# Attention and MLP kernel on one core: MLP weights split into f16 rows and turned by crossbar transposes instead of on TensorE

## The reference

```python
xn = layernorm(x)                                # x: [1, 2048, 512]
y  = x + attention(xn, Wq, Wkv, Wo, bo) + ffn(xn, gate, up, down)
# attention: 16 heads of 32, 4 key/value heads, causal, ALiBi bias
# ffn: W = lut[4-bit codes] * scales[row, block of 32]; gate, up: [4096, 512], down: [512, 4096]
inter = gelu_tanh(xn @ Wg.T) * (xn @ Wu.T);  ffn = inter @ Wd.T
```

## Time and profile before

| | us |
|---|---|
| median of 3 executions (1735.28 to 1737.32) | 1736.85 |
| the profiled execution | 1738.06 |
| its span in the profile | 1736.2 |
| TensorE busy in the span | 1666.9 (96%) |
| VectorE busy | 1312.1 (76%) |
| ScalarE busy | 1067.0 (61%) |
| GpSimd busy | 935.9 (54%) |

### The profile page before, as it was taken

One profiled execution on the slowest core, in us unless ns is written; L12 is line 12 of the kernel. 1 busy time (PEld: TensorE's weight loads), 2 busy tenths in 40 slices (PEclk: granted clock), 3 DMA queues, 4 the chain that ended last, 5 costly groups with the idle time before them and its releaser, 6 DMA issues.

```text
span 1736.2 us, 30755 instructions
## 1 busy us (share of the span) xinstructions
PE 1666.9 (96%) x10337; PEld 830.9 (48%) x10337; DVE 1312.1 (76%) x2782; ACT 1067.0 (61%) x1788; POOL 935.9 (54%) x807
## 2 busy tenths in 40 slices
PE   4989999999999999999999999999999999999998
PEld 3764444444444444444444444444444444444443
DVE  6767778777777777777777778777777778777755
ACT  2336757575666757575766757575767657575650
POOL 3304637465665747465655747464656647464650
PEclk9999999999999999999999999999999999999999
DMA  6761020202021020202021020202020120202135
GB/s 195 197 188 44 15 74 18 76 26 71 18 62 38 23 79 17 75 27 75 17 72 26 26 76 17 75 27 76 18 76 19 28 74 17 76 27 82 32 102 181
DMA packets 95843, 106.86 MB, mean 62 GB/s; under 512 B 38288, under 2 KB 63768, under 8 KB 93992
## 3 DMA queue, kind: packets, MB, share of 16 engines
q1 hardware_dynamic: 91368, 99.27, 20.6%
q10 hardware_dynamic: 4320, 5.64, 1.0%
HBM read 69.60 MB, written 22.42 MB: 53 GB/s over the span
## 4 chain that ended last, share of the span: by engine, by line
PE 74%; DVE 8%; issue 6%; ACT 5%; DMA 0%; POOL 0%; SPq 0%; POOLq 0%; DVEq 0%; ACTq 0%
PE up_ps L1233 16%; PE down_ps L1213 16%; PE gate_ps L1233 15%; PE o_ps L1276 8%; PE score_ps L1267 8%; PE max_ps L1245 4%; PE turn_ps L1245 3%; ACT p L1395 2%; DVE mxp L1526 2%; PE l_ps L1276 2%; ACT wh L354 1%; PE max_ps L347 1%; DVE score_ps L1511 1%; DVE gl L1482 1%; DVE acc L1473 1%
## 5 line engine op out<-in xcount | busy, mean ns | idle before, releaser
L1668 POOL TENSOR_TENSOR plo<-p,phi 128x512 f16<-128x512 f32 (+1 forms) x576 | 661.0, 1158 | 317.6 <-ACT phi L1402 316.3
L1395 ACT ACTIVATE p<-score_ps,pshift 128x512 f32<-128x512 f32 (+1 forms) x576 | 381.5, 662 | 284.3 <-DVE score_ps L1511 154.7
L1676 POOL TENSOR_TENSOR il<-prod,ih 128x512 f16<-128x512 f32 x128 | 160.4, 1253 | 371.1 <-DVE ih L1505 371.1
L1402 ACT ACTIVATE phi<-p 128x512 f16<-128x512 f32 (+1 forms) x576 | 349.5, 607 | 15.2
L1267 PE MATMUL score_ps<-qst,kst 128*128 128x512 f32 (+3 forms) x640 | 308.0, 497 | 20.5 <-ACT p L1395 18.8
L1526 DVE TENSOR_REDUCE mxp<-max_ps 128x1 f32<-128x512 f32 x256 | 175.5, 686 | 52.2 <-PE max_ps L1245 52.2
L1473 DVE TENSOR_TENSOR acc<-down_ps,acc 128x512 f32<-128x512 f32 x237 | 161.8, 683 | 62.4 <-PE down_ps L1213 62.1
L1233 PE MATMUL gate_ps<-xh,wh 128*128 128x512 f16 x512 | 198.8, 388 | 0.0
L1233 PE MATMUL up_ps<-xh,wh 128*128 128x512 f16 x512 | 197.9, 387 | 0.0
L1213 PE MATMUL down_ps<-wh,ih 128*128 128x512 f16 x506 | 195.8, 387 | 0.0
L1233 PE MATMUL gate_ps<-xh,wl 128*128 128x512 f16 x512 | 194.8, 380 | 0.0
(11 more groups left out here) (301 smaller groups left out, 2836.0 us busy)
## 6 DMA issues: line engine op xcount, KB each, us to landing
qst<-q_parts SPq DMA_DIRECT2D x192, 64.0 KB
o<-oraw SPq DMA_DIRECT2D x192, 64.0 KB, 2.0
kst<-k_parts SPq DMA_DIRECT2D x45, 256.0 KB, 6.0
vst<-v_parts SPq DMA_DIRECT2D x16, 512.0 KB, 6.1
q_parts<-o SPq DMA_DIRECT2D x24, 256.0 KB, 3.4
acc<-in_L_attn_x_dram SPq DMA_DIRECT2D x4, 1024.0 KB, 7.5
raw<-L_ffn_gate_W_packed_dram SPq DMA_DIRECT2D x16, 256.0 KB, 3.0
raw<-n_L_ffn_up_W_packed_dram SPq DMA_DIRECT2D x16, 256.0 KB, 3.1
```

What stands on the lines that cost most here:

```text
L1395: nc.scalar.activation(p32[n % PR][:, 0:cols], score_ps[:, 0:cols], ACT.Exp, bias=pshift[:, 0:1]).then_inc(exp_done, 1)
L1402: nc.scalar.activation(phi[n % PP][:, 0:cols], p32[n % PR][:, 0:cols], ACT.Copy).then_inc(phi_done, 1)
L1668: nc.gpsimd.tensor_tensor(plo[n % PP][:, 0:cols], p32[n % PR][:, 0:cols], phi[n % PP][:, 0:cols], ALU.subtract).then_inc(plo_done, 1)
L1676: nc.gpsimd.tensor_tensor(il[w % 2][:, a, :], prod[a][:], ih[w % 2][:, a, :], ALU.subtract).then_inc(il_done, 1)
```

## The change

The weights are split before they are turned. From `wf` ScalarE makes the f16 high rows of a whole matrix in one 128x1024 copy (`rows_hi`, slots 31, 36, 41, between exp and phi) into the bytes of `raw[m]`, and one slot later VectorE makes the low rows, `wf` minus the high rows, in one 128x1024 subtraction (`rows_lo`, slots 32, 37, 42, ahead of the slot's decode step) into part 1 of the previous head's output buffer `o3`. SP then turns both by crossbar transposes, one DMA of 256 KB each, straight into `wh` and `wl` (`turn_rows`, all three matrices between the blocks c = 2 and c = 3). TensorE's turns and the PSUM copies are gone.

New waits: `rows_lo` of m = 1 and 2 waits until both transposes of m - 1 have landed (one buffer of low rows); TensorE waits for the landing ahead of the first gate, up and down piece of a group; the raw loads wait for it too, since the high rows lie in `raw`. The factor that went into the down weights through `cur` now goes into `product`, whose scalar becomes a column of `cur` in place of a constant. The down codes come in two DMAs of half-rows. In the preamble the high rows are made on ScalarE at steps (2,4), (3,1), (3,4), the low rows on GpSimd after its last other work, and the transposes are in SP's list at (3,1), (3,3) and after the loop. In the last iteration nothing is made.

```diff
-TURN_W_AT = {31: (0, 0), 32: (0, 1), 36: (1, 0), 37: (1, 1), 41: (2, 0), 42: (2, 1)}
+ROWS_HI_AT = {31: 0, 36: 1, 41: 2}
+ROWS_LO_AT = {32: 0, 37: 1, 42: 2}
+W_DMAS = 2
...
+ROWS_FIRST_AT = {(2, 4): 0, (3, 1): 1, (3, 4): 2}
+TURN_FIRST_AT = {(3, 1): 0, (3, 3): 1}
...
+    def rows_hi(act, m, before):
+        act.wait_ge(wf_done, before * 6 + 2 * m + 2)
+        nc.scalar.activation(hi_rows[m], wf[:], ACT.Copy).then_inc(rowhi_done, 1)
+
+    def rows_lo(eng, m, before, lo_row):
+        eng.wait_ge(rowhi_done, before * 3 + m + 1)
+        eng.tensor_tensor(lo_row, wf[:], hi_rows[m], ALU.subtract).then_inc(rowlo_done, 1)
+
+    def turn_rows(sp, m, before, b, lo_row):
+
+        for done, rows, dst in ((rowhi_done, hi_rows[m], wh[b]), (rowlo_done, lo_row, wl[b])):
+            sp.wait_ge(done, before * 3 + m + 1)
+            sp.dma_start_transpose(dst[:, m].rearrange("p a (k n) -> p (a k) n", n=P), rows).then_inc(w_in[m], 16)
...
+                        if i < LAST and c == 2:
+                            for m, used in enumerate((gate_done, up_done, down_done)):
+                                sp.wait_ge(used, after(i * (GU if m < 2 else ND)))
+                                turn_rows(sp, m, i + 1, 1 - par, lo_rows[1 - par])
                     if i + 2 < HEADS:
                         for m in range(3):
-                            sp.wait_ge(wf_done, (i + 1) * 6 + 2 * m + 2)
+                            sp.wait_ge(w_in[m], 16 * W_DMAS * (i + 2))
                             load_raw(sp, m, i + 2)
...
                             if q == 0:
                                 pe.wait_ge(gelu_done if m == 0 else prod_done, after(i * GU + n))
+                                if n == 0:
+                                    pe.wait_ge(w_in[m], 16 * W_DMAS * (i + 1))
...
-                        nc.vector.scalar_tensor_tensor(prod[a][:], gl[a][:], 0.5 * IS / (XS * WS) ** 2, up_ps[:],
+                        nc.vector.scalar_tensor_tensor(prod[a][:], gl[a][:], cur[par][:, 4 + a:5 + a], up_ps[:],
...
+                        if s in ROWS_LO_AT:
+                            m = ROWS_LO_AT[s]
+                            if i:
+                                dve.wait_ge(osum_done, 2 * i)
+                            else:
+                                dve.wait_ge(acc_done, after(1))
+                            if m:
+                                dve.wait_ge(w_in[m - 1], 16 * W_DMAS * (i + 2))
+                            rows_lo(nc.vector, m, i + 1, lo_rows[1 - par])
```

More of the change, by code:

```diff
@@ L337, in decode_step @@
                 ALU.mult).then_inc(wf_done, 1)
[L339 to L350, removed]
-        act.wait_ge(wturn_done, before * 6 + 2 * m + a + 1)
-        if m == 2:
-            act.wait_ge(cur_done, before + 1)
-        nc.scalar.activation(wh[b][:, m, a, :], banks[a][:], ACT.Copy,
-                             scale=1.0 if m < 2 else cur[b][:, 4 + a:5 + a]).then_inc(wh_done, 1)
-    def weights_lo(dve, m, a, before, b):
-        dve.wait_ge(wh_done, before * 6 + 2 * m + a + 1)
-        nc.vector.scalar_tensor_tensor(wl[b][:, m, a, :], banks[a][:], 1.0 if m < 2 else cur[b][:, 4 + a:5 + a],
-                                       wh[b][:, m, a, :], ALU.mult, ALU.subtract).then_inc(wl_done, 1)
-    return load_raw, decode_step, turn_weights, weights_hi, weights_lo
+    def rows_hi(act, m, before):
[8 more added lines that the diff above has]
+            sp.dma_start_transpose(dst[:, m].rearrange("p a (k n) -> p (a k) n", n=P), rows).then_inc(w_in[m], 16)
+    return load_raw, decode_step, rows_hi, rows_lo, turn_rows
 def preamble(nc, e):
@@ L470, in preamble @@
         CLEARED = 3
-        load_raw, decode_step, turn_weights, weights_hi, weights_lo = weight_steps(nc, e, w_ps)
+        load_raw, decode_step, rows_hi, rows_lo, turn_rows = weight_steps(nc, e)
+        lo_rows = [t.bitcast(F16) for t in sraw]
         QSCALE = float(np.float32(1 / np.sqrt(np.float32(HD))))
@@ L608, in _ @@
                 nc.gpsimd.partition_all_reduce(rall, rmax, P, RMAX).then_inc(rall_done, 1)
+                for m in range(3):
+                    rows_lo(nc.gpsimd, m, 0, lo_rows[m])
             @block.tensor
@@ L724, in _ @@
                             root(c + 2)
-                        if (c, j) in TURN_FIRST_AT:
-                            for a in range(2):
-                                weights_hi(act, TURN_FIRST_AT[c, j], a, 0, 0)
+                        if (c, j) in ROWS_FIRST_AT:
+                            rows_hi(act, ROWS_FIRST_AT[c, j], 0)
                     act.wait_ge(v_sum, c + 1)
@@ L1102, in _ @@
                     sp.wait_ge(stored, 32 * NCH)
-                for m in range(3):
-                    load_raw(sp, m, 1)
                 def body(i, par, pair):
@@ L1114, in body @@
                     if i == 0:
+                        for m in range(3):
+                            sp.wait_ge(w_in[m], 16 * W_DMAS)
+                            load_raw(sp, m, 1)
                         sp.wait_ge(os_out, 16)
```

90 lines of the change are left out of this document (40 added, 50 removed).

## The result

The changed kernel takes 1765.33 us (median of 4 executions, 1764.16 to 1766.71) against 1736.76 for the kernel before, run beside it: a ratio of 1.0167 [1.0151, 1.0183], 28.6 us slower. The forecast was 1732.5 us, 0.2% faster. The time lies in the range (1700 to 1780), on the wrong side of no change.

What follows compares the result with a forecast made beforehand. The prediction took TensorE (busy 96% of the span) as the bound, with ScalarE nearly as full in slots 31 to 39. Loop -9.0, product +1.1, preamble +3.6 sum to -4.3 us: 1732.5 us from 1736.85, range 1700 to 1780.

Steps and rivals of the forecast that it cites:

- TensorE's turns: Loop, slots 31 to 43: removal worth 39.6 us if TensorE alone set the pace; 0.1 us back in slots 31 to 40.
- ScalarE's new place at slot 31: One larger copy between exp and phi delays exp(33); the next slot's score starts at 776.8, 0.37 us later than before.
- 0.37 for a subtraction of 1.6: Slots 41 to 44: the score of slot 44 comes 0.37 us earlier if VectorE's subtraction takes 1.6 us, 0.75 if 1.2.
- the main loop's -9.0: Main loop: 0.6 us gained an iteration in slots 41 to 44, times 15, -9.0 us; ends 0 and 2.64 an iteration.
- retiming: One iteration's operations moved in each engine's order, keeping their busy start distances, to get new score times in slots 31 to 44.
- the next scores are within 0.1 us of the old times until slot 39: After slot 36: exp(37) moves back 0.7 us, the two turns dropped there make up for it.
- 96.7: Main loop: an iteration should take 96.7 us in place of 97.3.
- The product: Its scalar as a column costs 0.07 us more each; one of eight on the path, +1.1 us, ends 0 and 9.
- The preamble: Before the main loop: six more DMA issues on SP's path at 0.6 us each, +3.6 us; ends 0 and 13.5.
- The transposes late: Rival: VectorE's rows_lo at slots 37 and 42 waits for landings; 1797 us at 6.5 us each, up to 2180; chance 0.25.
- the interpolated 5.4: Loop: landing time in us of one 256 KB transpose, taken as 1024 pieces of 256 B; hidden, so no cost.
- The costs without the gain: Rival: transfers in time, but ScalarE takes the gain of slots 41 to 44 or SP's issues cost more; +15, about 1750; 0.12.

Runs made afterwards that it cites:

- Experiment 3: Kernel before, three of the four transposes of each TensorE turn in the main loop left out, copies as many as ever: 1730.23 us, ratio 0.997.
- experiment 6: Changed kernel, low rows filled in the main loop by two VectorE multiplications by 0 reading PSUM, in place of the subtraction from SBUF: 1731.99 us, 0.9976.
- experiment 8: Changed kernel with the rows of m = 1 one slot later and the head's output work moved to slots 45 to 47: 1743.19 us, 1.0039.
- Experiments 7 and 9: 7: kernel before, low weights subtracted from SBUF, 1743.22 us (cleared instead: 1730.76). 9: changed kernel, weight work spread over more slots, 1760.75 (kernel before, output also moved: 1728.05).
- experiment 11: Changed kernel with plain copies of the same 256 KB in place of the crossbar transposes: 1758.92 us, 1.0137.
- experiment 12: Changed kernel, preamble transposes issued from ScalarE's queue: 1766.18 us; or those of m = 1 and 2 moved behind head 0's loads on SP: 1766.38 us.
- experiments 5 and 6: 5: changed kernel, low rows cleared by a VectorE memset in the main loop, 1723.34 us. 6: low rows filled by pieces reading PSUM, 1731.99 us.

## Why the prediction was wrong, point by point

**TensorE's turns: worth little. Right.** 39.6 us of turns went, at the prediction's price, and TensorE waited 43 us more for exps. Experiment 3 shows it in the kernel before, without the rest of the change.

**ScalarE's new place at slot 31: right to 0.1 us.** The score of slot 34 came where it was retimed. In slots 41 to 44 too: from the score of slot 41 to that of slot 44 it was 6.16 us before and 5.77 after, a gain of 0.39, where I had 0.37 for a subtraction of 1.6.

**The term that failed is the main loop's -9.0.** It priced VectorE's subtraction by its own length, and that length was right. (It also booked 0.6 us an iteration where its own retiming for that length gives 0.37, that is 5.6 us in all.) It did not price what a long operation with two SBUF sources does to GpSimd beside it, and GpSimd to VectorE's other work. I had seen the effect in the trace of before (679 to 1761 ns in one line) and used it for the length of the new instruction alone. Two engines share that contention. The Trainium skill says so ("VectorE: DVE Perf Modes", on two Vector instructions with no wait between them: the second SBUF read goes through an interface shared with GpSimd), and the trace agrees: the `plo` beside the subtraction of slot 32 takes 1.55 us, beside the pieces that read PSUM 1.16. The prediction quoted it and carried it into one row only. What came in its place, in slots 36 to 40: decode steps of 1.38 and 1.56 us, `wf` late, and the high-row copy standing 1.39 us with exp(37) behind it. The retiming said "the next scores are within 0.1 us of the old times until slot 39", and slot 38 came 1.1 us late. Then GpSimd's multiply of 2.25 us, and another 0.5 us behind `onh`. Less the 0.39 that makes about 1.25 us an iteration by the timeline; the main loop shows 1.4.

**How large it is: experiment 6.** With pieces of 1.37 us that read PSUM, the changed kernel takes 1732.0 us. From its first maximum to the end it needs 1730.0 - 129.31 = 1600.7 us, the kernel before 1736.2 - 123.62 = 1612.6: 12 us gained in the loop, where loop and product together were forecast at 7.9. An iteration takes 96.5 us there (exp to exp, median), where 96.7 was forecast; in the changed kernel 98.7. So the retiming was sound for an operation that leaves GpSimd alone; the sources of the subtraction cost the 33 us that were missing. That two ways bind together, the late `wf` and the late GpSimd, is shown by experiment 8. Experiments 7 and 9 show that the price depends on which instructions are lengthened, and not on how much in sum; how large it is at a given place stays open.

**The product: right in size.** 742 ns in the median (734 to 750) where a constant took some 680; the 1.1 us on the path is compatible with the 1.4 measured, and with nothing.

**The preamble: mis-sized.** 3.6 us forecast, 6.3 in the profile, 5.7 by experiment 11. Both carry an error of a few microseconds: with the same preamble the first maximum starts between 128.4 and 130.3 us in the profiles of the changed kernel and its variants, and between 121.7 and 125.1 in those of the kernel before. SP's timeline of the kernel after:

```profile
107.49 1.57 SPq L359 DMA_TRANSPOSE wh<-raw  x1
109.11 2.60 SPq L359 DMA_TRANSPOSE wl<-acc  x1
...
128.73 0.43 SPq L556 DMA_DIRECT2D column_scales<-acc  x1
```

The issue of a transpose takes 1.30 to 2.60 us here (1.23 at best in the loop), not the 0.6 of a plain one. The sum of the six, 10.0 us, was within the ends (0 to 13.5), and I took the near row without asking what the issue of a strided transfer in blocks costs. Moving them (experiment 12) gained nothing: behind head 0's loads the first `up` matmul waits for them, and from ScalarE's queue the main loop started later.

**The transposes late: fell.** DMA issues of the kernel after (count, median us from issue to landing):

```profile
wh<-raw SPq DMA_TRANSPOSE x48, 3.1
...
wl<-o SPq DMA_TRANSPOSE x45, 2.8
```

3.1 and 2.8 us, less than the interpolated 5.4. Of the two rules of the Trainium skill the 1309 ns for one 128x128 block ("VectorE: DVE Perf Modes", the three transpose paths) does not hold as a serial price here: eight blocks would be an estimated 10.5 us. The rate of 261 GB/s ("DMA: Bandwidth & Descriptors", latency and other measured facts; an estimated 1 us plus a fixed part) is compatible with the landing.

**The costs without the gain**, which I gave 0.12, had the right direction and was too cheap (1750): it let ScalarE take the gain, and had no place for a loss inside the loop.

## What to carry to other kernels

A VectorE operation with two SBUF sources beside a busy GpSimd has two prices, its own length and what it does to both engines' other work. Ask what stands at the head of an in-order queue waiting for either, and retime the stretch with those lengths too. The sum of busy time does not give the price: look at which instructions start while the other engine works. Two engines late side by side hide each other: when single moves give nothing (-2 and +3 us), try them together (-22) before the theory is dropped. And an operand's place can be tested alone, at nearly the same length of instruction, as in experiment 6.

## What was not expected of the hardware

- The decode steps have one SBUF source each, and their length moves by a factor of two to four with what stands elsewhere in VectorE's and GpSimd's lists: 0.36 and 0.69 us with the low rows cleared, 1.38 and 1.56 in the same slots of the changed kernel. The groups by line (count, busy us, mean ns, idle before), of the kernel before and then of that of experiment 6:

```profile
L326 DVE TENSOR_SCALAR dec<-dec 128x1024 int32<-128x1024 int32 x48 | 44.7, 932 | 0.1
L322 DVE TENSOR_SCALAR dec<-raw 128x512 int32<-128x512 int32 x48 | 43.8, 913 | 0.0
```

```profile
L329 DVE TENSOR_SCALAR dec<-raw 128x512 int32<-128x512 int32 x48 | 42.4, 883 | 0.0
L333 DVE TENSOR_SCALAR dec<-dec 128x1024 int32<-128x1024 int32 x48 | 38.4, 799 | 0.1
```

  In the changed kernel the means are 1074 (L333) and 1054 ns (L329), with the rows cleared 888 and 532. The means mix two cases. In the timelines of these four kernels a step of these two lines in the main loop that starts with GpSimd idle takes 0.36 to 0.42 us (512 columns) or 0.68 to 0.69 (1024); one that starts while a GpSimd instruction runs takes 0.83 to 1.50 or 1.05 to 1.57. Of the 45 steps of 1024 columns 15 start beside GpSimd in the kernel before and in experiments 5 and 6, and 30 in the changed one. An estimate from a mean can't see that move.
- The issue of a 256 KB transpose holds the issuing queue for 1.24 us in the median, 1.23 at best and 3.29 at most, on ScalarE's queue 1.3 to 2.7. The plain copies of the same bytes in experiment 11 take 0.46 in the median and 1.21 at most.
- 256 KB turned by the crossbar land in 3 us, as fast as the plain loads of 256 KB in 1 KB pieces; the plain copies of experiment 11 land in 2.3.
- Against cleared rows, three subtractions per iteration from SBUF cost 42 us in the one kernel, six from PSUM 5 in the other.
